# Three rounded products for an attention output projection, and two copies that change engines

## What is computed

```
y = num / (den[..., None] + 1e-06)
mu = mean(y, axis=-1); var = mean((y - mu) ** 2, axis=-1)
y = (y - mu) / sqrt(var + 1e-09) * ln_w
attn = y.reshape(B, T, 1024) @ w_proj          # the output projection
x = x + ga * attn
h = layernorm(x) * (1 + cb) + sb
logits = h @ Wr.T                              # 8 numbers a token, choose the experts
```

## Time and profile before

| | us |
|---|---|
| median of 3 runs | 2179.81 (2179.35 to 2181.45) |
| the profiled execution | 2178.68 |
| its span in the trace | 2176.9 |
| stage of the change, about 1346 to 1573 us of the span | 227 |
| TensorE busy | 1995.8 (92%) |
| vector engine busy | 1803.1 (83%) |
| ScalarE busy | 1294.1 (59%) |
| GpSimd busy | 781.8 (36%) |
| mean granted clock of TensorE | 0.954 |

### The profile page before, as it was taken

One profiled execution on the slowest core, in us unless ns is written; L12 is line 12 of the kernel. 1 busy time (PEld: TensorE's weight loads), 2 busy tenths in 40 slices (PEclk: granted clock), 3 DMA queues, 4 the chain that ended last, 5 costly groups with the idle time before them and its releaser, 6 DMA issues. The chain is left out here.

```text
span 2176.9 us, 37910 instructions
## 1 busy us (share of the span) xinstructions
PE 1995.8 (92%) x13199; PEld 1365.7 (63%) x13199; DVE 1803.1 (83%) x2652; ACT 1294.1 (59%) x2168; POOL 781.8 (36%) x729
## 2 busy tenths in 40 slices
PE   7999689999999999999999996899726999999994
PEld 5677434444444444544444443789625999999994
DVE  6999769999999999999999997777587778777783
ACT  4444367777777777777777774344303656566661
POOL 3777501111111111111111111466525666666663
PEclk9999789999999999999999998999956999999997
DMA  5887883235543244543255402344332333444444
GB/s 191 286 275 270 272 203 82 80 101 122 126 120 72 82 112 122 121 104 81 78 126 122 121 20 69 95 134 131 117 107 68 83 71 80 87 86 88 88 85 107
DMA packets 156104, 260.57 MB, mean 120 GB/s; under 512 B 44568, under 2 KB 120160, under 8 KB 149472
## 3 DMA queue, kind: packets, MB, share of 16 engines
q1 hardware_dynamic: 127792, 214.07, 35.3%
q0 software_dynamic: 15840, 22.29, 6.5%
q10 hardware_dynamic: 12304, 22.02, 3.1%
HBM read 162.40 MB, written 100.14 MB: 121 GB/s over the span
## 5 line engine op out<-in xcount | busy, mean ns | idle before, releaser
L980 ACT ACTIVATE att_sb_a<-att_ps_s,att_sb_fg,att_sb_f 128x1024 f32<-128x1024 f32 x384 | 458.7, 1203 | 286.3 <-PE att_ps_s L1117 272.5
L1018 DVE TENSOR_TENSOR keep_sb_store<-keep_sb_store,att_sb_a 128x1024 f32<-128x1024 f32 (+1 forms) x528 | 533.1, 1036 | 34.5 <-ACT att_sb_a L980 32.6
L936 POOL TENSOR_SCALAR_AFFINE_SELECT att_sb_dec<-att_sb_dec 128x128 f32<-128x128 f32 x256 | 130.1, 508 | 941.4 <-ACT att_sb_dec L970 941.4
L1136 PE MATMUL att_ps_off<-att_sb_a,att_sb_v 128*64 128x512 f32 x1520 | 389.0, 601 | 0.1
L1117 PEld LDWEIGHTS att_ps_s<-keep_sb_late,att_sb_k 64*128 64x128 f32 x1920 | 158.4, 185 | 159.0 <-issue 86.7
L1117 PEld LDWEIGHTS att_ps_s<-att_sb_q,att_sb_k 64*128 64x128 f32 x1896 | 157.2, 186 | 160.4 <-issue 89.1
L1769 ACT ACTIVATE ffn_sb_h<-ffn_ps_p,ffn_sb_b_cols 128x256 f32<-128x256 f32 x320 | 151.7, 476 | 169.3 <-PE ffn_ps_p L1960 168.4
L1117 PE MATMUL att_ps_s<-att_sb_q,att_sb_k 64*128 64x512 f32 (+2 forms) x1896 | 243.7, 381 | 3.5 <-DMA att_sb_k<-k_rows 3.5
L1117 PE MATMUL att_ps_s<-keep_sb_late,att_sb_k 64*128 64x512 f32 (+3 forms) x1920 | 246.8, 381 | 0.0
L1034 DVE SCALAR_TENSOR_TENSOR att_sb_a<-att_ps_s,att_sb_dec 128x1024 f32<-128x1024 f32 (+3 forms) x256 | 209.7, 819 | 41.0 <-PE att_ps_s L1117 36.8
L1874 DVE TENSOR_TENSOR ffn_sb_h_lo<-ffn_sb_h,ffn_sb_h_hi 128x256 fp32r<-128x256 f32 x320 | 213.0, 708 | 28.1 <-ACT ffn_sb_h_hi L1762 26.8
(11 more groups left out here) (256 smaller groups left out, 3583.7 us busy)
## 6 DMA issues: line engine op xcount, KB each, us to landing
q_rows<-early_sb_halves SPq DMA_DIRECT2D x32, 1024.0 KB, 4.9
att_sb_k<-k_rows SPq DMA_DIRECT2D x60, 512.0 KB, 15.8
ffn_sb_raw<-L_ffn_W ACTq DMA_DIRECT2D x36, 512.0 KB, 4.0
close_sb_nT<-num_rows SPq DMA_DIRECT2D x34, 512.0 KB, 4.0
k_rows<-early_sb_halves SPq DMA_DIRECT2D x16, 1024.0 KB, 4.9
keep_sb_late<-q_rows SPq DMA_DIRECT2D x32, 512.0 KB, 14.0
num_rows<-att_sb_num SPq DMA_DIRECT2D x64, 256.0 KB, 2.5
att_sb_hb<-half_log SPq DMA_DIRECT2D x15, 1024.0 KB, 22.8
```

The costliest lines, as they stand in the source:

```text
L936: nc.gpsimd.affine_select(out=tile, in_=tile, compare_op=ALU.is_ge, fill=0.0, base=0, pattern=[[1, P]], channel_multiplier=-1).then_inc(de ...
L980: nc.scalar.activation(x, s_ps[slot(op)][:, :, :], ACT.Square, scale=f[:, p, i - 1, s:s + 1], bias=fg[:, p, i - 1, s:s + 1]).then_inc(sq_d ...
L1018: nc.vector.tensor_tensor(x[:, :, c:TB], x[:, :, c:TB], y[:, :, c:TB], ALU.max).then_inc(max_done, 1)
L1136: last = nc.tensor.matmul(ps[h * HD:(h + 1) * HD, c:TB], v_tile, a[:, a_slot(op), h, c:TB], start=(s == 0), stop=(s == (ST * i if kind == ...
```

## The change

The projection's plain fp32 product becomes three products of rounded operands: `w` is kept as `w_hi` (rounded to fp32r) and `w_lo` (the rest), `yT` as `yT_hi` and `yT_lo`; `pa` is `yT_hi*w_hi + yT_hi*w_lo + yT_lo*w_hi`, 24 matmuls instead of 8. ScalarE's copy of `py` writes `yT_hi`. The vector engine makes `yT_lo` = `py` - `yT_hi` (128x1024) at the end of its turn, and `w_lo` in each part of `fold`. The copy of the logits goes from the vector engine's turn, before L1373, to the end of ScalarE's turn. TensorE's transposes into `py` and its projection wait for `yT_lo` instead of `yT`.

```
         def _(act):
                 if there[2]:
                     act.wait_ge(y_mm, ready(n - 2))
                     act.wait_ge(a_mm, free(n - 2, 2))
-                    nc.scalar.activation(yT[:, p, :, :], py[:, :, :], ACT.Copy).then_inc(yT_done, 1)
+                    nc.scalar.activation(yT_hi[:, p, :, :], py[:, :, :], ACT.Copy).then_inc(yT_hi_done, 1)
...
+                if there[7]:
+                    act.wait_ge(l_mm, ready(n - 7))
+                    apart(act, keep)
+                    nc.scalar.activation(keep.logits[:, n - 7, :], pl[:, :], ACT.Copy).then_inc(l_done, 1)
...
                 for g in parts:
+                    at = slice(2 * g, 2 * g + 2)
                     dve.wait_ge(fold_mm, g + 1)
-                    nc.vector.tensor_copy(w[:, 2 * g:2 * g + 2, :], pw[:, :, :]).then_inc(folded, 1)
+                    nc.vector.tensor_copy(w_hi[:, at, :], pw[:, :, :]).then_inc(rounded, 1)
+                    dve.wait_ge(rounded, g + 1)
+                    nc.vector.tensor_tensor(w_lo[:, at, :], pw[:, :, :], w_hi[:, at, :].bitcast(F32), ALU.subtract).then_inc(folded, 1)
...
-                if there[7]:
-                    dve.wait_ge(l_mm, ready(n - 7))
-                    apart(dve, keep)
-                    nc.vector.tensor_copy(keep.logits[:, n - 7, :], pl[:, :]).then_inc(l_done, 1)
...
                     nc.vector.reciprocal(rinv[:, p, :], red[:, 4, :]).then_inc(r_done, 1)
+                if there[2]:
+                    dve.wait_ge(yT_hi_done, ready(n - 2))
+                    dve.wait_ge(a_mm, free(n - 2, 2))
+                    nc.vector.tensor_tensor(yT_lo[:, p, :, :], py[:, :, :], yT_hi[:, p, :, :].bitcast(F32),
+                                            ALU.subtract).then_inc(yT_lo_done, 1)
...
                 if there[2]:
                     pe.wait_ge(y_done, ready(n - 2))
-                    pe.wait_ge(yT_done, free(n - 2, 1))
+                    pe.wait_ge(yT_lo_done, free(n - 2, 1))
...
                 if there[3]:
-                    pe.wait_ge(yT_done, ready(n - 3))
+                    pe.wait_ge(yT_lo_done, ready(n - 3))
                     pe.wait_ge(gx_done, free(n - 3, 1))
-                    for j in range(KVH):
-                        last = nc.tensor.matmul(pa[:, :], yT[:, 1 - p, j, :], w[:, j, :], start=(j == 0), stop=(j == KVH - 1))
+                    terms = [(a, b, j) for a, b in ((yT_hi, w_hi), (yT_hi, w_lo), (yT_lo, w_hi)) for j in range(KVH)]
+                    for o, (a, b, j) in enumerate(terms):
+                        last = nc.tensor.matmul(pa[:, :], a[:, 1 - p, j, :], b[:, j, :], start=(o == 0), stop=(o == len(terms) - 1))
                     last.then_inc(a_mm, 1)
```

More of the change, by code:

```diff
@@ L1155, in close_attention @@
         w_raw = m.sbuf("w_raw", [P, KVH, D])
-        w = m.sbuf("w", [P, KVH, D])
+        w_hi = m.sbuf("w_hi", [P, KVH, D], F32R)
+        w_lo = m.sbuf("w_lo", [P, KVH, D], F32R)
         basis_sb = m.sbuf("basis", [P, P])
@@ L1167, in close_attention @@
         y = m.sbuf("y", [P, 2, HEADS, HD])
-        yT = m.sbuf("yT", [P, 2, KVH, P])
+        yT_hi = m.sbuf("yT_hi", [P, 2, KVH, P], F32R)
+        yT_lo = m.sbuf("yT_lo", [P, 2, KVH, P], F32R)
         gx = m.sbuf("gx", [P, 2, D])
@@ L1183, in close_attention @@
         pw = m.psum("pw", [P, 2, D])
-        w_in, scaled, fold_mm, folded, wr_mm, wr_done, eps_done = (
-            m.sem(s) for s in ("w_in", "scaled", "fold_mm", "folded", "wr_mm", "wr", "eps"))
+        w_in, scaled, fold_mm, rounded, folded, wr_mm, wr_done, eps_done = (
+            m.sem(s) for s in ("w_in", "scaled", "fold_mm", "rounded", "folded", "wr_mm", "wr", "eps"))
         n_in = [m.sem(f"n_in{i}") for i in range(2)]
@@ L1188, in close_attention @@
         h_out = [m.sem(f"h_out{i}") for i in range(2)]
-        n_mm, num_done, sq_done, var_done, std_done, r_done, y_done, y_mm, yT_done, a_mm = (
-            m.sem(s) for s in ("n_mm", "num", "sq", "var", "std", "r", "y", "y_mm", "yT", "a_mm"))
+        n_mm, num_done, sq_done, var_done, std_done, r_done, y_done, y_mm, yT_hi_done, yT_lo_done, a_mm = (
+            m.sem(s) for s in ("n_mm", "num", "sq", "var", "std", "r", "y", "y_mm", "yT_hi", "yT_lo", "a_mm"))
         gx_done, x1_done, var2_done, std2_done, xn_done, hs_done, h2_done, h_mm, hT_done, l_mm, l_done, head_chain, norm_chain, mod_chain = (
@@ L1248, in _ @@
         def _(act):
-            for s in (sq_done, std_done, yT_done, std2_done, hT_done):
+            for s in (sq_done, std_done, yT_hi_done, std2_done, hT_done, l_done):
                 act.sem_inc(s, CREDIT)
@@ L1271, in turn @@
                     nc.scalar.activation(red[:, 4, :], red[:, 3, :], ACT.Sqrt).then_inc(std_done, 1)
+                if there[7]:
+                    act.wait_ge(l_mm, ready(n - 7))
+                    apart(act, keep)
+                    nc.scalar.activation(keep.logits[:, n - 7, :], pl[:, :], ACT.Copy).then_inc(l_done, 1)
             turns(act, turn)
+            act.wait_ge(l_done, ready(NTT - 1))
         @block.gpsimd
@@ L1307, in _ @@
         def _(dve):
-            for s in (num_done, var_done, r_done, gx_done, var2_done, xn_done, l_done):
+            for s in (num_done, var_done, r_done, gx_done, var2_done, xn_done, yT_lo_done):
                 dve.sem_inc(s, CREDIT)
```

## The result

The changed kernel takes 2204.03 us (median of 4 runs, 2201.29 to 2204.55), against 2180.18 us of the kernel before: 23.9 us more, a ratio of 1.0106 with a 95% interval of 1.0089 to 1.0124. The forecast was 2211.5 us, the range 2198 to 2226 us. The sign and the place are right, the forecast loss is about a third too large. The profiled execution took 2204.3 us, its span is 2202.5 us, 25.6 us more than before.

A forecast was written before the change was run, and what follows sets the result against it. The prediction took the vector engine's chain over ScalarE and TensorE to be both at the bound. Loop +25.4, turns 2 to 7 +6.9, fold +1.25, tail -1.9 made +31.7 on 2179.8: 2211.5 us, range 2198 to 2226.

The forecast's parts named there:

- a full bound already: Loop: the vector engine with its round trip over ScalarE fills the 5.94 us turn; TensorE's turn is about as long.
- The sum of 6.00 us: Loop before: the vector engine's chain from `gx` to `gx` adds up to 6.00 us, within 1% of the 5.94 us turn.
- Not one of the large gaps names TensorE: Loop before: large vector engine gaps are waits for ScalarE (0.22 us), "issue" (0.12 us), or between operations feeding each other.
- The loop's term: Loop, 24 turns: the new chain takes 7.00 us a turn, 1.06 more than 5.94, so +25.4 us.
- the chain over `py`: Loop rival: `yT_lo`, `py`, ScalarE's copy, `sq` end last instead of hidden by 0.20 us; 2222 to 2234 us, 10%.
- The low bound of 2202 us: Whole kernel: each "issue" gap of the loop's chain goes beneath `yT_lo`, -0.4 us a turn, 2202 us.
- Turns 3 to 7: Written-out turns ahead of the loop: 1.15 us more each, five times 1.15 = 5.75 us.
- The fold and turn 2: Fold: three subtractions cost 2.4 us, some 1.15 come back, net +1.25; turn 2: +1.15 us.
- The tail: After the loop: TensorE sets the pace, three projections each shorter by 0.63 us, -1.9 us.
- TensorE as the pace: Loop rival: the vector engine's idle 1.24 us a turn is slack that takes the new work; 2175 us, 5%.
- The clock: Loop rival: TensorE's pauses drop its clock to 1.2 GHz, up to +108 us, 2320 us at worst; 5%.
- The rounded matmuls: Projection: 0.117 us each, 24 in 2.82 us; rival, the fp32 records' rate, 5.2 us and 2230 us, 2%.

The follow-up runs named there:

- e3: Kernel before plus one vector operation of `yT_lo`'s shape and waits, result unused, projection plain fp32, logits' copy unmoved: 2205.37 us beside 2184.36, ratio 1.0102.
- e2: Changed kernel without `yT_lo`, the third product taking `yT_hi` again (low part missing): 2184.23 us beside 2184.36 of before, ratio 1.0003.
- e1: Kernel before with only the logits' copy moved from the vector engine to the end of ScalarE's turn: 2186.64 us beside 2184.36, ratio 1.0012.
- e5: Changed kernel with `yT_lo` moved from before `gx` to right behind `num`: 2207.28 us beside 2182.28 of before, ratio 1.0111.
- e4: Changed kernel with ScalarE's order changed, `sq` ahead of `yT_hi`: 2202.27 us beside 2184.36 of before, ratio 1.0090.
- e9: Kernel before with ScalarE's order alone changed, `sq` ahead of `yT`: 2183.98 us beside 2182.28, ratio 1.0003.
- e7: Changed kernel without `yT_lo` (`yT_hi` instead), `gx` behind `num`, `sq` first on ScalarE, one `pa` buffer: 2209.52 us, ratio 1.0127 to before.

## Why the prediction was right, and where its size was off

**What bounds the loop.** Right in what decides the case: new work on the vector engine lengthens the turn (e3, +0.65 us), less work on TensorE gives nothing (e2 against e1). Not right in calling the vector engine with its round trip "a full bound already". The sum of 6.00 us took the `gx` to `num` of both halves of the loop as its own, and 0.25 us of one half are a wait for TensorE's `pn`; it also took `num` to `sq` from the longer half alone (1.36, mean 1.31). Its own chain is 5.81 us of the 5.94. "Not one of the large gaps names TensorE" held for the names only: the gap before L1355 was called "issue" and isn't in the earlier trace rows. And the ring over `hT`, `pl`, `py` was nearly as long, and appears as soon as something is added to it (e1).

**The loop's term, +25.4 us; measured 24 x 0.685 = 16.4 us** (from `gx` to `gx`; the 16.9 us of the table begin at `num` 8)**.** This is the mis-sized term. By its own steps: `gx` to `num` was put at 1.26, it is 0.90 us. I had taken away the "issue" gap before `gx` (0.12 us), but left the one before L1355, 0.27 us a turn. Of it 0.13 us were the wait for `pn`, gone with the longer turn. The rest is work of the sequencer: with `yT_lo` ahead of `gx` the distance from `gx` to L1355 is 0.33 us, without it 0.55 (e5). `rinv` to `yT_lo` 0.16 for 0.27 us, `yT_lo` to `gx` 1.08 for 1.15: the operation lasts 1.16 us, not the 1.21 of L485. Against that, `num` to `sq` is 1.40 for 1.26 us: 0.10 us because the chain over `py` ends last, 0.04 us because it is 1.30 us even with `sq` first (e4, e9). And L1373 to `rinv` 2.02 for 1.99. Sum: -0.36 - 0.11 - 0.07 + 0.14 + 0.03 = -0.37 us, 7.00 down to 6.63. The low bound of 2202 us was made of nearly this, "if each issue gap goes beneath `yT_lo`"; it should have been the forecast.

**Turns 3 to 7**: five times 1.15 = 5.75 us said, 5.4 measured. Right.

**The fold and turn 2**, +1.25 and +1.15 = 2.4 us said, 3.8 measured. The subtractions take 0.69 us each, L1321 (before: L1314) took 0.28 us as forecast. The surplus is another operation:

```profile
1357.09 1.90 POOL L1308 TENSOR_TENSOR close_sb_y<-close_sb_num,close_sb_rinv 128x1024 f32<-128x1024 f32 x1 [11.10 <-DVE close_sb_rinv L1392]
1357.21 2.86 DVE L1337 TENSOR_SCALAR close_sb_w_raw<-close_sb_w_raw,close_sb_lnw 128x2048 f32<-128x2048 f32 x1 [0.21 <-DMA close_sb_wr_raw<-L_ffn_Wr]
```

In the profiled run of before the scaling of `w_raw` began at 1356.15, 0.17 us ahead of GpSimd's `y`, and took 1.21 us (`y` then took 2.80 us instead of 1.90); here it began 0.12 us behind `y`, since it waited for a transfer, and took 2.86 us. The change has no part in it: in e1, e3 and e9, with the fold of before, it starts behind `y` as well and `num` 0 to `num` 3 takes 30.2 to 30.3 us instead of 28.3. Against those the changed kernel's 32.12 us are +1.9 us, for 2.4 said.
The Trainium skill (VectorE: DVE Perf Modes, section "Two Vector instructions with no wait between them") calls the second SBUF read interface of the vector engine shared with GpSimd. The trace fits something shared: the scaling ended 2.98 us after `y` began, 1.08 us after its end, which leaves nearly its whole 1.21 us behind `y`. Which interface it reads through no run here shows.

**The tail**, -1.9 us said, -0.7 measured. The projections are shorter as said, but the clock fell when the loop ended: after pauses of 1.36 and 0.56 us the granted clock was 0.50 (1.2 GHz) from 1575.4 to 1578.8, and the transposes and the first third of the projection ran at half the rate.

```profile
1575.49 1.94 PE L1440 MATMUL close_ps_py<-keep_sb_ident,close_sb_y 128*128 128x128 f32 x8 [0.56 <-DVE close_sb_yT_lo L1396]
1577.08 1.95 PE L1447 MATMUL close_ps_pa<-close_sb_w_hi,close_sb_yT_hi 128*128 128x256 f32 x8
1578.87 1.10 PE L1447 MATMUL close_ps_pa<-close_sb_w_lo,close_sb_yT_hi 128*128 128x256 f32 x8
```

From 1575.49 to 1578.87 are 3.38 us; a loop turn does the same in 1.84 us (1502.58 to 1504.42): 1.5 us lost, more than the miss of 1.2. I had priced the clock's fall as a rival for the loop and not for the tail.

**The rivals.** TensorE as the pace: the vector engine's gaps held 0.13 us a turn of waits for TensorE, far from the 1.0 us that this rival needed, and e3 loses with TensorE's work unchanged. The chain over `py`: it did end last, for 0.1 us a turn (e4), inside a turn that was shorter than I thought for another reason. The clock: stayed at 1.00 in the loop with TensorE busy for 84%, idle for 1.03 us a turn (1.5 or more said). The rounded matmuls: 0.117 us each as forecast, and 0.93 us from one eight to the next.

## What to carry to other kernels

An engine that is busy for 99% of a loop can still have almost nothing to give: add up the start-to-start distances around the loop for the engine with the smaller share too, and if they make up nearly the whole turn, new work there costs nearly its full length, whatever it saves elsewhere. A gap that the profile calls "issue" can hold a wait: compare its distance to the other engine's operation with a run where the wait is named. And before the new operation is added at its length, look at the gaps of the sequencer beside it: those behind a short operation vanish when a long one takes its place, here 0.22 of 1.08 us, and 0.13 us more was a wait that the longer turn filled. An order that fills a wait is only as good as the number of buffers behind it: with one `pa`, moving `gx` made the loop 1.4 us longer; with two it took 0.5 us a turn off the changed kernel, together with ScalarE's new order.

## What the runs showed of the hardware that I had not expected

A vector subtraction of PSUM minus SBUF, 128x1024, took 1.16 us in the loop where an operation of the same shape took 1.21, and the next started 1.08 us after it. A vector operation on SBUF alone (`w_raw`, 128x2048) took 1.21 and 1.26 us where it began 0.17 us before GpSimd's `y` (before, e7), which then took 2.80 and 2.85 us instead of 1.90. In the other twelve traces it began between 0.03 us before `y` and 0.62 us behind it, took 2.37 to 3.01 us, and always ended 2.98 or 2.99 us after `y` began: in the first case `y` ended 1.76 us behind the scaling's end, in the others the scaling 1.08 us behind the end of `y`, so the second of the two did most of its work only when the first had ended. In most of these traces the profile names the transfer of `wr_raw` as what the scaling had waited for, and the two orders differ by 1.7 us in the scaling.
